# Expert layers of a graph network: first-layer weights split during the attention, new places for the weight tiles, and the best experts found by maximum and first index

## The chip, the cores and the metric

The kernel runs on one core of one Trainium2 chip. The metric is the device time of that core in microseconds. The kernel before takes 1104.51 us (median of three runs, 1102.79 to 1106.34). The core's engines run side by side and meet at semaphores: TensorE (PE in the profile) multiplies matrices, VectorE (DVE), ScalarE (ACT) and GpSimd (POOL) work on vectors, and SyncE (SP) issues transfers. GpSimd also issues the indirect transfers, which gather and scatter rows by an index.

## What is computed

Four blocks act in turn on x, 1024 nodes by 512 features, each on the normalised rows and each added to x. The second and the fourth end in a mixture of eight experts. For these the change alters how the work is ordered; of what is computed only the choice of the experts is written in another way.

```python
x = x + _L0_gnn_ref(_layernorm(x), ...)   # masked attention over 1024 nodes
x = x + _L0_ffn_ref(_layernorm(x), ...)   # experts, the best 2 of 8
x = x + _L1_gnn_ref(_layernorm(x), ...)   # sum over neighbours, two layers
x = x + _L1_ffn_ref(_layernorm(x), ...)   # 8-head attention, then experts, the best 1 of 8

# experts of L0
raw_weights = softmax(flat_x @ gate_w + gate_b)
top_w, top_idx = top_k(raw_weights, 2)
h = gelu(einsum('td,edh->teh', flat_x, w1) + b1)       # w1: 8 x 512 x 256
expert_out = einsum('teh,ehd->ted', h, w2) + b2        # w2: 8 x 256 x 512
combined = einsum('ted,te->td', expert_out, gate_output)
# experts of L1
idx = argmax(t @ Wg + bg)
```

`top_k` and `argmax` take the expert with the lower index where two are equal.

## The kernel before

**Three passes.** A product in full precision is made of three TensorE passes (`three_pass`, L324). Each operand is split into a high part, which is its copy in the rounded type fp32r, and a low part, the operand minus that copy. For the expert weights, `W1R` and `W2R` hold what was loaded (512 KB an expert and layer), `W1H` and `W2H` the high parts, and `W1L` and `W2L` the low parts, written over what was loaded. ScalarE makes the high parts (`w1_hi`, `w2_hi`). VectorE makes the low parts (`weights_lo`, recorded as L971), except the first `POOL_LO` of the first layer's, which GpSimd makes (`expert_lo`, L553): 3 in the first expert layer and 6 in the second. One subtraction of an expert's weights is a 128x1024 instruction.

**An expert layer (`moe`) has a head and a loop.** In the head the normalised rows `XN` are transposed on TensorE (`PS`), copied by ScalarE to `LTH`, and subtracted by VectorE to `LTL`. TensorE multiplies them with the split gate weights `gws`, ScalarE copies the logits to `gatesT`, and TensorE transposes them back (`gt_ps`). VectorE then ranks the eight logits of each row: it compares every expert with every other (`cmp4`, five instructions of 128x512 over 8 tiles x 8 x 8), counts, and writes `picked`. TensorE sums `picked` to ranks and totals. VectorE works out from these which slot each row takes, in blocks of 128 rows for one expert each, and writes `gather_i` and `scatter_i`. Only then can GpSimd gather the first rows (`BX`). The loop follows, 23 blocks in the first layer and 15 in the second: transposed rows, first layer (`hidden`), bias (`hidden_bias`, tile `BH`, L1327), gelu, second layer, scatter. TensorE sets its pace.

**The order is written by hand.** Each engine runs its own list, in order; a wait holds back everything behind it on that engine. VectorE's list in a head is: `LTL` x8, in the first layer the low part of `gws`, then `weights_lo(7)`, the gating, one more subtraction ahead of the slots, and the rest (5 in the first layer, 2 in the second) between the slots and the first rows of the loop.

**What lies ahead of the heads.** The first head follows the masked attention, eight tiles of 128 rows, each with a mask and a minimum on VectorE (`SM`, semaphores `m1` and `m2`), an exponential on ScalarE (`PR`), transposes, `PTH` and `PTL`, the product with V on TensorE, and the addition to x (`residual`, L1169). `W1R` lies where the scores `SR` lay, a slice of 4 KB a partition for each expert as for each tile; its loads wait until all eight tiles are masked. The second head follows the 8-head attention. There, normalisation (`norm_root`, L987 to L996, instructions of 128x8) and `scaled_rows` (L1556, L1560) make `XN`. The tile named WH in ScalarE's rows of L931 is the context's high part, which uses part of the weights' room.

## Time and profile before

| | before |
|---|---|
| median of three runs | 1104.51 us |
| the profiled execution | 1104.55 us, its span 1102.8 us |
| TensorE busy | 884.4 us (80% of the span) |
| VectorE busy | 764.6 us (69%) |
| ScalarE busy | 506.7 us (46%) |
| GpSimd busy | 360.4 us (33%) |
| chain that ended last | PE 57%, DVE 34%, ACT 4% |

By stretches (us from the span's start), with the mean granted clock of TensorE as a share of 2.4 GHz:

| stretch | PE busy | DVE busy | clock |
|---|---|---|---|
| 240 to 310, masked attention | 57.13 | 44.19 | 0.95 |
| 310 to 352, head of the first expert layer | 14.35 | 38.42 | 0.64 |
| 352 to 437, its loop | 82.58 | 35.88 | 0.98 |
| 437 to 655, sums over neighbours | 175.54 | 112.35 | 0.87 |
| 655 to 950, 8-head attention | 264.54 | 222.32 | 0.98 |
| 950 to 1008, norm and head of the second expert layer | 19.04 | 50.89 | 0.64 |
| 1008 to 1066, its loop | 54.23 | 27.36 | 0.97 |

A busy engine is not by that the one that sets the time; what does is read from the chain of waits, which goes back from the last instruction to what released it, step by step. In the timelines, a row is a group of like instructions on one engine. The bracket behind it is the time for which the engine had nothing to do before it, and what ended that wait. Records overlap a little: an instruction's own duration is longer than the distance to the next start.

### The profile page before, as it was taken

The page shows a single profiled execution, that of the slowest core. Times are in us where ns is not written, and L with a number is a line of the kernel's source. Part 1 is how long each engine was busy: PE and PEld are TensorE (multiplying, and loading weights), DVE is VectorE, ACT ScalarE, POOL GpSimd, SP SyncE. Part 2 cuts the span into 40 slices and gives each one's busy share as a digit, 9 for nine tenths or more (in the row PEclk, how much of TensorE's full clock was granted, in tenths as well). Part 3 has the DMA queues.
Part 4 walks back from the last instruction along what each step waited for, and adds up shares of the span by engine and source line. Part 5 has one row for each costly group of instructions (what it writes and reads, how often), then busy time and mean ns, then how long its engine had stood idle before and what let it go on. Part 6 is the DMA issues. An engine that isn't in the chain of part 4 may idle for free.

```text
span 1102.8 us, 13781 instructions
## 1 busy us (share of the span) xinstructions
PE 884.4 (80%) x4522; PEld 675.1 (61%) x4522; DVE 764.6 (69%) x1545; ACT 506.7 (46%) x880; POOL 360.4 (33%) x238
## 2 busy tenths in 40 slices
PE   2999998878953999298898789999999888445990
PEld 2877773337742887077686567777777666334860
DVE  8879599886687443856122767787777776895638
ACT  3467527655362554132302146666665655542530
POOL 1000000000023453007330337786785766602520
PEclk9999999999985999589998999999999998966985
DMA  5010000013371444423110320020010230552442
GB/s 157 29 22 1 1 1 1 1 56 137 113 268 48 135 153 143 163 96 102 52 53 14 105 77 1 20 58 20 1 29 20 72 101 1 168 203 63 151 147 90
DMA packets 55523, 84.74 MB, mean 77 GB/s; under 512 B 8976, under 2 KB 31760, under 8 KB 54944
## 3 DMA queue, kind: packets, MB, share of 16 engines
q1 hardware_dynamic: 49376, 63.94, 18.3%
q0 software_dynamic: 6080, 19.93, 5.5%
q8 instruction: 39, 0.64, 0.2%
q14 instruction: 28, 0.23, 0.1%
HBM read 57.11 MB, written 22.54 MB: 72 GB/s over the span
## 4 chain that ended last, share of the span: by engine, by line
PE 57%; DVE 34%; ACT 4%; issue 3%; POOL 1%; DMA 1%; DVEq 0%; ACTq 0%; POOLq 0%
PE PS L324 37%; DVE late_columns L1133 4%; PE PS L1915 3%; PE PS L1930 3%; DVE neg_max L1488 3%; PE PS L1904 3%; DVE APL L971 2%; PE PS L1929 2%; DVE count_rows L1113 2%; PE PS L1823 2%; PE PS L1604 2%; PE PS L1766 2%; DVE early_columns L1133 1%; DVE XN L1004 1%; DVE stats L979 1%
## 5 line engine op out<-in xcount | busy, mean ns | idle before, releaser
L611 POOL TENSOR_SCALAR AP__193<-AP__193,rden 128x1024 f32<-128x1024 f32 x64 | 181.9, 2847 | 86.4 <-DVE rden L1493 85.7
L553 POOL TENSOR_TENSOR W1L<-W1R,W1H 128x1024 fp32r<-128x1024 f32 x9 | 21.0, 2362 | 307.3 <-ACT W1H L643 307.3
L643 ACT ACTIVATE APH<-PS 128x512 fp32r<-128x512 f32 x128 | 71.7, 597 | 70.1 <-PE PS L1915 45.7
L1488 DVE TENSOR_REDUCE neg_max<-PS 128x1 f32<-128x1024 f32 x64 | 78.2, 1222 | 36.9 <-PE PS L1904 36.0
L971 DVE TENSOR_TENSOR APL<-PS,APH 128x512 fp32r<-128x512 f32 x128 | 82.9, 679 | 23.8 <-ACT APH L643 23.5
L324 PE MATMUL PS<-XTH,WH 128*128 128x512 f32 x224 | 81.5, 411 | 4.5 <-DVE XTL L971 4.5
L1915 PE MATMUL PS<-ident,AP__193 128*128 128x128 f32 x512 | 71.2, 281 | 11.6 <-DVE APL L971 10.8
L324 PE MATMUL PS<-XTL,WH 128*128 128x512 f32 x224 | 78.1, 396 | 0.0
L324 PE MATMUL PS<-XTH,WL 128*128 128x512 f32 x224 | 77.8, 394 | 0.0
L1915 PEld LDWEIGHTS PS<-ident,AP__193 128*128 128x128 f32 x512 | 59.9, 144 | 28.3 <-issue 17.2
L914 ACT ACTIVATE AP__193<-PS,neg_max 128x1024 f32<-128x1024 f32 x64 | 71.5, 1117 | 7.3 <-DVE neg_max L1488 6.6
L544 POOL CAST WH<-RAW 128x512 fp32r<-128x512 f32 x30 | 23.7, 789 | 156.2 <-PE PS L324 91.7
L563 POOL DMA_INDIRECT BX<-normalised,gather_i x38 | 40.2, 1057 | 90.0 <-DVE scatter_i L1311 70.6
L1080 DVE SCALAR_TENSOR_TENSOR edge_lanes<-lanes,edge_lane,edge_vals 128x256 f16<-128x256 f16 x136 | 55.6, 478 | 8.0 <-PE PS L1604 8.0
L1583 PE MATMUL PS<-ident,XN 128*128 128x128 f32 x128 | 28.3, 399 | 40.8 <-DVE XN L1004 16.1
L1930 PE MATMUL PS<-APH,AV 128*128 128x512 f32 x128 | 50.9, 398 | 9.9 <-DVE APL L971 9.7
L576 POOL DMA_INDIRECT expert_rows<-BY,scatter_i x38 | 37.4, 985 | 60.5 <-ACT BY L643 60.5
L676 ACT ACTIVATE edge_steps<-blocks,edge_step 128x145 f16<-128x145 f16 x136 | 45.3, 408 | 20.5 <-PE PS L1604 16.9
L1583 PEld LDWEIGHTS PS<-ident,XN 128*128 128x128 f32 x128 | 23.3, 209 | 45.9 <-DVE XN L1004 17.8
L971 DVE TENSOR_TENSOR BHL<-PS,BHH 128x256 fp32r<-128x256 f32 x38 | 16.1, 424 | 50.4 <-ACT BHH L643 50.4
L1133 DVE TENSOR_SCALAR late_columns<-columns,block_rc 128x512 f16<-128x512 f16 x189 | 50.5, 348 | 0.0
L324 PEld LDWEIGHTS PS<-XTH,WH 128*128 128x128 f32 x224 | 42.1, 193 | 13.3 <-POOL WL L546 3.5
(297 smaller groups left out, 2423.4 us busy)
## 6 DMA issues: line engine op xcount, KB each, us to landing
YT<-expert_rows SPq DMA_DIRECT2D x12, 512.0 KB, 6.8
counts<-CT SPq DMA_DIRECT2D x8, 512.0 KB, 4.9
W1R<-in_L_ffn_w SPq DMA_DIRECT2D x8, 512.0 KB, 8.7
W2R<-in_L_ffn_w SPq DMA_DIRECT2D x8, 512.0 KB, 5.3
normalised<-XN SPq DMA_DIRECT2D x2, 2048.0 KB, 8.0
CG<-counts SPq DMA_DIRECT2D x8, 512.0 KB, 3.3
RAW<-in_L_gnn_W SPq DMA_DIRECT2D x16, 256.0 KB, 2.7
W1R<-in_L_ffn_W SPq DMA_DIRECT2D x8, 512.0 KB, 8.6
```

Of the source, the lines that this page charges most:

```text
L324: got = pe.matmul(o, lhs, r, start=first and j == 0, stop=last and j == 2)
L611: gp.tensor_scalar(AP_[:, i % 4, :], AP_[:, i % 4, :], rden[:, i % 4:i % 4 + 1], None, ALU.mult).then_inc(B["norm"], 1)
L643: act.activation(dst, src, Copy, **kw).then_inc(s, 1)
L676: got = act.activation(edge_steps[:, q % 2, j, 0:STEPS_OF], blocks16[:, :], ACT.Sign, bias=edge_step[:, 4 * q + j:4 * q + j + 1])
L914: act.activation(AP_[:, i % 4, :], banks(2 * (i % 2)), ACT.Exp, bias=neg_max[:, i % 4:i % 4 + 1], accum_out=denom[:, i % 4:i % 4 + 1]).the ...
L971: v.tensor_tensor(dst, src, f(hi), ALU.subtract).then_inc(s, 1)
L1080: got = v.scalar_tensor_tensor(out=edge_lanes[:, q % 2, j, :, :], in0=lanes1[:, :].unsqueeze(1).to_broadcast([P, 2, P]), scalar=edge_lane[ ...
L1133: got = v.tensor_scalar(count_columns(k, j), columns16[:, r * HALF:(r + 1) * HALF], block_rc[:, 1, b:b + 1], None, ALU.is_equal)
L1488: v.tensor_reduce(out=neg_max[:, i % 4:i % 4 + 1], in_=banks(2 * (i % 2)), axis=X_AXIS, op=ALU.max, negate=True).then_inc(B["mx"], 1)
L1583: got = pe.transpose(PS[:, t % 4, k * P:(k + 1) * P], src[:, t, k * P:(k + 1) * P], ident[:, :])
L1915: got = pe.transpose(PS[:, 4 + half, k * P:(k + 1) * P], AP_[:, i % 4, c * P:(c + 1) * P], ident[:, :])
L1930: got = pe.matmul(PS[:, 6, :], AV[:, hp % 2, h, k, :], APH[:, k, :], start=k == 0, stop=k == NT - 1)
```

## The change

- **Gate weights.** Their high part (ScalarE) is made in the attention, and their low part (VectorE) before the last two `residual`.
- **Loads.** `W1R[e]` of the first expert layer is loaded once tile e of the attention is masked, rather than all eight after the last.
- **High parts.** In the first layer ScalarE makes `W1H` 0 to 3 between two exponentials of the attention and 4 to 7 right after it. In the second layer it makes 0 to 3 ahead of the last context copy (L931) and 4 to 7 behind it.
- **Homes.** `W1H` of the first layer lies where the attention's weights lay, and `W2H` where `W1H` was. In the second layer both stay.
- **Low parts.** In the first layer VectorE makes its five `W1L` before the last two `residual` (2 and 3). Behind `LTL` stand 2 subtractions (second layer: 3) instead of 7, then one behind `gates`, one ahead of the slots, 3 (4) behind the slots, and the last 1 (2) behind the loop's first two `BTL`. GpSimd makes 3 and 5 of the first layer's, and waits in the first for the last minimum (`m2`).
- **Best experts.** No comparison of all pairs: the maximum, the experts equal to it, times `rank8` (8 down to 1), the maximum of that, and the expert whose rank it is. For the second best, the first is pushed to minus 3.0e38 and the same is done again. Probabilities get their own tile `prob`.
- **Setup.** `rank8` (an iota of 8 elements) takes the place of `lower` (a memset and an affine_select of 64).

The order of instructions shows the moves at three places. First, VectorE at the end of the masked attention (PTL is the low part of the transposed probabilities, X the `residual`, stats and mv its statistics, eps a constant of the next block). Before:

```order
L971 TENSOR_TENSOR PTL<-PS,PTH 128x1024
L1169 SCALAR_TENSOR_TENSOR X<-PS,rden,X 128x512
L979 BN_STATS stats<-X 128x6
L981 BN_AGGR mv<-stats 128x2
L1169 SCALAR_TENSOR_TENSOR X<-PS,rden,X 128x512
L979 BN_STATS stats<-X 128x6
L981 BN_AGGR mv<-stats 128x2
L1400 TENSOR_SCALAR eps_70<-eps_70 128x1
```

And now:

```order
L976 TENSOR_TENSOR PTL<-PS,PTH 128x1024
L976 TENSOR_TENSOR gws<-gw,gws 128x8x8
L976 TENSOR_TENSOR W1L<-W1R,W1H_156 128x1024 x2
L1174 SCALAR_TENSOR_TENSOR X<-PS,rden,X 128x512
L984 BN_STATS stats<-X 128x6
L986 BN_AGGR mv<-stats 128x2
L976 TENSOR_TENSOR W1L<-W1R,W1H_156 128x1024 x3
L1174 SCALAR_TENSOR_TENSOR X<-PS,rden,X 128x512
L984 BN_STATS stats<-X 128x6
L986 BN_AGGR mv<-stats 128x2
```

The gate weights' low part and five subtractions of W1 now stand between the last `PTL` and the last `X`.

Second, VectorE in the second head, from the last `LTL` to the slots (cmp is `cmp4`, best, top and top_key the new small tiles, over the first tile of the slots). Before:

```order
L971 TENSOR_TENSOR LTL<-PS,LTH 128x4x128 x8
L971 TENSOR_TENSOR W1L<-W1R,W1H 128x1024 x2
L971 TENSOR_TENSOR W2L<-W2R,W2H 128x1024 x5
L1214 TENSOR_TENSOR gtmp<-PS,gbias 128x64
L1217 TENSOR_TENSOR gtmp<-PS,gtmp 128x64
L1237 TENSOR_TENSOR cmp_171<-gtmp 128x512
L1238 TENSOR_TENSOR cmp_171<-gtmp 128x512
L1240 TENSOR_TENSOR cmp_171<-cmp_171,lower 128x512
L1242 TENSOR_TENSOR cmp_171<-cmp_171 128x512
L1244 TENSOR_REDUCE gates<-cmp_171 128x64
L1251 TENSOR_SCALAR picked<-gates 128x64
L1256 TENSOR_SCALAR gates<-gates 128x64
```

And now:

```order
L976 TENSOR_TENSOR LTL<-PS,LTH 128x4x128 x8
L976 TENSOR_TENSOR W1L<-W1R,W1H_157 128x1024 x3
L1218 TENSOR_TENSOR gtmp<-PS,gbias 128x64
L1221 TENSOR_TENSOR gtmp<-PS,gtmp 128x64
L1228 TENSOR_REDUCE best<-gtmp 128x8
L1230 TENSOR_TENSOR top<-gtmp,best 128x64
L1235 TENSOR_TENSOR top_key<-top,rank_76 128x64
L1237 TENSOR_REDUCE best<-top_key 128x8
L1272 TENSOR_TENSOR picked<-rank_76,best 128x64
L1273 TENSOR_TENSOR gates<-rank_76,best 128x64
L976 TENSOR_TENSOR W2L<-W2R,W2H_161 128x1024
L1283 TENSOR_TENSOR over<-PS,edges_97 128x64
```

Four of seven subtractions are gone from between LTL and the gating, the five 128x512 instructions are gone, and one subtraction stands behind `gates`.

Third, ScalarE at the end of the 8-head attention (APH is the high part of the transposed probabilities, WH the context's copy). Before:

```order
L643 ACTIVATE APH<-PS 128x4x128 x6
L931 ACTIVATE WH<-PS,BVA 64x512
L643 ACTIVATE W1H<-W1R 128x1024 x8
L648 ACT_TABLE_LOAD
L648 ACTIVATE rstd<-ve 128x8
L643 ACTIVATE LTH<-PS 128x4x128 x8
```

And now:

```order
L647 ACTIVATE APH<-PS 128x4x128 x6
L647 ACTIVATE W1H_157<-W1R 128x1024 x4
L934 ACTIVATE WH<-PS,BVA 64x512
L647 ACTIVATE W1H_157<-W1R 128x1024 x4
L652 ACT_TABLE_LOAD
L652 ACTIVATE rstd<-ve 128x8
L647 ACTIVATE LTH<-PS 128x4x128 x8
```

Four of the copies to `W1H` have moved ahead of the last context copy.

The diff, cut to its core:

```diff
-    STEPS = (37, 22)
-    POOL_LO = (3, 6)
+    STEPS = (42, 21)
+    POOL_LO = (3, 5)
...
-        def load_w1(w1):
+        def load_w1(which, w1):
             for e in range(NEXP):
+                if which == 0:
+                    wait(A["m1"], e + 1)
                 sp.dma_start(W1R[:, e, :, :], w1[e].rearrange("(k p) h -> p k h", p=P)).then_inc(M["w_in"][e // 4], 16)
...
-        wait(A["m1"], NT)
-        load_w1(a["L0_ffn_w1"])
+        load_w1(0, a["L0_ffn_w1"])
...
 
+        wait(A["m2"], NT)
         expert_lo(0)
         expert_rows(0)
...
+        def w1_hi(which, e):
+            act.wait_ge(M["w_in"][e // 4], which * (160, 96)[e // 4] + 64)
+            copy(W1H[which][:, e, :, :], W1R[:, e, :, :], M["w_hi"])
+
         no_edge(0, 0)
         no_edge(0, 1)
         softmax(0, 0)
@@ -759,39 +767,34 @@
         p_hi(0, 0)
         for i in range(NT // 2 - 1):
             no_edge(i + 1, 0)
+            if i == 1:
+                act.wait_ge(cols_in, 16 * 11)
+                copy(gws[:, :, :, 0:NEXP], gw[:, :, :, :], gw_hi)
+            if i == 2:
+                w1_hi(0, 0)
+                w1_hi(0, 1)
             softmax(i + 1, 0)
             p_hi(i, 1)
...
+            if i == 2:
+                w1_hi(0, 2)
+                w1_hi(0, 3)
...
-
-            if which == 0:
-                act.wait_ge(A["m2"], NT)
-                act.wait_ge(A["stored"], 16 * NT)
-            for e in range(4 if which == 0 else NEXP):
-                w1_hi(e)
+                copy(W2H[which][:, e, :, :], W2R[:, e, :, :], M["w_hi"])
+
+            for e in range(4, NEXP):
+                w1_hi(which, e)
             root((1, 4)[which])
-            if which == 0:
-                w1_hi(4)
-                w1_hi(5)
-                act.wait_ge(A["av_ps"], NT)
-                w1_hi(6)
-                w1_hi(7)
             transposed(turn, LTH)
             if which == 0:
-                act.wait_ge(cols_in, 16 * 11)
...
                         v_hi(hp + 1, m - 10)
+        for e in range(4):
+            w1_hi(1, e)
         context_hi(4 * KT - 1)
...
+        low_tasks = [[(1, e) for e in range(POOL_LO[m], NEXP)] + [(2, e) for e in range(NEXP)] for m in range(2)]
+
+        def weights_lo(which, n):
+            for _ in range(n):
+                layer, e = low_tasks[which].pop(0)
+                v.wait_ge(M["w_hi"], 2 * NEXP * which + NEXP * (layer - 1) + e + 1)
+                wl, wr, wh = ((W1L, W1R, W1H[which]), (W2L, W2R, W2H[which]))[layer - 1]
+                lo(wl[:, e, :, :], wr[:, e, :, :], wh[:, e, :, :], M["w_lo_dve"])
+
...
         p_lo(NT // 2 - 1, 1)
+        v.wait_ge(gw_hi, 1)
+        lo(gws[:, :, :, NEXP:2 * NEXP], gw[:, :, :, :], gws[:, :, :, 0:NEXP], gw_ready)
+        weights_lo(0, 2)
         residual(NT // 2 - 1, 0)
+        weights_lo(0, 3)
         residual(NT // 2 - 1, 1)
...
         def moe(turn, which, acc):
             transposed(turn, LTH, LTL)
...
-            weights_lo(7)
+            weights_lo(which, 2 + which)
...
+            order = rank8[:, :].unsqueeze(1).to_broadcast([P, NT, NEXP])
+            own(v.tensor_reduce(out=best[:, 0, :], in_=gtmp[:, :, :], axis=X_AXIS, op=ALU.max))
+            v.wait_ge(M["gate_dve"], steps[0])
+            own(v.tensor_tensor(top[:, :, :], gtmp[:, :, :], wide(best[:, 0, :]), ALU.is_equal))
+            seen = steps[0]
             if which == 0:
-                own(v.tensor_reduce(out=gsum[:, :], in_=gtmp[:, :, :], axis=X_AXIS, op=ALU.max))
+                own(v.tensor_tensor(prob[:, :, :], gtmp[:, :, :], wide(best[:, 0, :]), ALU.subtract))
+            v.wait_ge(M["gate_dve"], seen)
+            own(v.tensor_tensor(top_key[:, :, :], top[:, :, :], order, ALU.mult))
+            v.wait_ge(M["gate_dve"], steps[0])
+            own(v.tensor_reduce(out=best[:, 1, :], in_=top_key[:, :, :], axis=X_AXIS, op=ALU.max))
+            v.wait_ge(M["gate_dve"], steps[0])
+            if which == 0:
+                own(v.tensor_tensor(first[:, :, :], order, wide(best[:, 1, :]), ALU.is_equal))
                 v.wait_ge(M["gate_dve"], steps[0])
-                own(v.tensor_tensor(gtmp[:, :, :], gtmp[:, :, :], wide(gsum[:, :]), ALU.subtract))
+                own(v.scalar_tensor_tensor(out=rest[:, :, :], in0=first[:, :, :], scalar=-3.0e38, in1=gtmp[:, :, :],
+                                           op0=ALU.mult, op1=ALU.add))
+                v.wait_ge(M["gate_dve"], steps[0])
+                own(v.tensor_reduce(out=best[:, 2, :], in_=rest[:, :, :], axis=X_AXIS, op=ALU.max))
+                seen = steps[0]
                 v.wait_ge(M["g_exp"], 1)
-                own(v.tensor_reduce(out=gsum[:, :], in_=gtmp[:, :, :], axis=X_AXIS, op=ALU.add))
+                own(v.tensor_reduce(out=gsum[:, :], in_=prob[:, :, :], axis=X_AXIS, op=ALU.add))
+                v.wait_ge(M["gate_dve"], seen)
+                own(v.tensor_tensor(top[:, :, :], rest[:, :, :], wide(best[:, 2, :]), ALU.is_equal))
+                v.wait_ge(M["gate_dve"], seen + 1)
+                own(v.reciprocal(gsum[:, :], gsum[:, :]))
+                v.wait_ge(M["gate_dve"], seen + 2)
+                own(v.tensor_tensor(top_key[:, :, :], top[:, :, :], order, ALU.mult))
+                v.wait_ge(M["gate_dve"], seen + 3)
+                own(v.tensor_tensor(prob[:, :, :], prob[:, :, :], wide(gsum[:, :]), ALU.mult))
+                v.wait_ge(M["gate_dve"], seen + 4)
+                own(v.tensor_reduce(out=best[:, 3, :], in_=top_key[:, :, :], axis=X_AXIS, op=ALU.max))
                 v.wait_ge(M["gate_dve"], steps[0])
-                own(v.reciprocal(gsum[:, :], gsum[:, :]))
+                own(v.tensor_tensor(second[:, :, :], order, wide(best[:, 3, :]), ALU.is_equal))
                 v.wait_ge(M["gate_dve"], steps[0])
-                own(v.tensor_tensor(gtmp[:, :, :], gtmp[:, :, :], wide(gsum[:, :]), ALU.mult))
-                v.wait_ge(M["gate_dve"], steps[0])
-            shape = [P, NT, NEXP, NEXP]
-            mine = gtmp[:, :, :].unsqueeze(3).to_broadcast(shape)
-            other = gtmp[:, :, :].unsqueeze(2).to_broadcast(shape)
-            own(v.tensor_tensor(cmp4[:, 0], other, mine, ALU.is_gt))
-            own(v.tensor_tensor(cmp4[:, 1], other, mine, ALU.is_equal))
-            v.wait_ge(M["gate_dve"], steps[0])
-            own(v.tensor_tensor(cmp4[:, 1], cmp4[:, 1], lower[:, :, :].unsqueeze(1).to_broadcast(shape), ALU.mult))
-            v.wait_ge(M["gate_dve"], steps[0])
-            own(v.tensor_tensor(cmp4[:, 0], cmp4[:, 0], cmp4[:, 1], ALU.add))
-            v.wait_ge(M["gate_dve"], steps[0])
-            own(v.tensor_reduce(out=gates[:, :, :], in_=cmp4[:, 0], axis=X_AXIS, op=ALU.add))
-            v.wait_ge(M["gate_dve"], steps[0])
-            K_, nb, first = CHOICES[which], BLOCKS[which], which * BLOCKS[0]
+            K_, nb, base = CHOICES[which], BLOCKS[which], which * BLOCKS[0]
             KN = K_ * NT
             mine8 = picked[:, (NT - 1) * NEXP:].rearrange("p (t e) -> p t e", t=NT)
             if which == 0:
                 v.wait_ge(tabled, 4)
-            v.tensor_scalar(mine8, gates[:, :, :], float(K_), None, ALU.is_lt).then_inc(M["routed"], 1)
             if which == 0:
-                v.scalar_tensor_tensor(out=gates[:, :, :], in0=gates[:, :, :], scalar=2.0, in1=gtmp[:, :, :],
-                                       op0=ALU.is_lt, op1=ALU.mult).then_inc(M["gates"], 1)
+                v.tensor_tensor(mine8, first[:, :, :], second[:, :, :], ALU.add).then_inc(M["routed"], 1)
+                v.wait_ge(M["routed"], 1)
+                v.tensor_tensor(gates[:, :, :], prob[:, :, :], mine8, ALU.mult).then_inc(M["gates"], 1)
             else:
...
+                v.tensor_tensor(mine8, order, wide(best[:, 1, :]), ALU.is_equal).then_inc(M["routed"], 1)
+                v.tensor_tensor(gates[:, :, :], order, wide(best[:, 1, :]), ALU.is_equal).then_inc(M["gates"], 1)
+            weights_lo(which, 1)
...
-            weights_lo(len(tasks))
+            weights_lo(which, 3 + which)
...
+            weights_lo(which, len(low_tasks[which]))
```

The other lines follow from these: `f(W1H[which])` and `W2H[which]` for the two homes, `base` for the name `first`, 12 for 13 steps of setup.

## Rows read from the trace of the kernel before

**Rows 1.** Timeline, VectorE, end of the first attention: start us, us, instruction, idle before.

```profile
303.02 0.75 DVE L1169 SCALAR_TENSOR_TENSOR X<-PS,rden,X 128x512 f32<-128x512 f32 x1 [3.04 <-PE PS L324]
...
308.46 0.75 DVE L1169 SCALAR_TENSOR_TENSOR X<-PS,rden,X 128x512 f32<-128x512 f32 x1 [3.74 <-PE PS L324]
```

**Rows 2.** Chain of waits, first expert head: start us, us, what.

```profile
320.91 5.67 DVE W1L L971 x5
```

**Rows 3.** Timeline, VectorE, first head.

```profile
328.78 0.21 DVE L1214 TENSOR_TENSOR gtmp<-PS,gbias 128x64 f32<-128x64 f32 x1
329.03 0.22 DVE L1217 TENSOR_TENSOR gtmp<-PS,gtmp 128x64 f32<-128x64 f32 x1
...
334.33 0.20 DVE L1251 TENSOR_SCALAR picked<-gates 128x64 f16<-128x64 f32 x1
334.44 0.22 DVE L1253 SCALAR_TENSOR_TENSOR gates<-gates,gtmp 128x64 f32<-128x64 f32 x1
335.43 0.23 DVE L1265 TENSOR_TENSOR over<-PS,edges 128x64 f32<-128x64 f32 x1 [0.76 <-PE PS L1744]
...
355.28 0.42 DVE L1327 TENSOR_TENSOR BH<-PS,B 128x256 f32<-128x256 f32 x1 [1.36 <-PE PS L324]
```

**Rows 4.** Timeline, TensorE, first head.

```profile
320.97 0.40 PE L1728 MATMUL PS<-LTH,gws 128*16 128x512 f32 x1 [1.86 <-DVE gws L971]
...
325.52 0.42 PE L1734 MATMUL PS<-ident,gatesT 16*128 16x16 f32 x4 [0.33 <-ACT gatesT L643]
```

**Rows 5.** Timeline, ScalarE, end of the first attention.

```profile
286.32 1.15 ACT L745 ACTIVATE PR<-SM,neg_max 128x1024 f32<-128x1024 f32 x1 [4.28 <-DVE neg_max L1152]
...
296.44 1.02 ACT L643 ACTIVATE PTH<-PS 128x1024 fp32r<-128x1024 f32 x1 [0.50 <-PE PS L1691]
```

**Rows 6.** Timeline, DMA queue of SyncE; DMA issues with median us to landing.

```profile
292.51 8.39 SPq L381 DMA_DIRECT2D W1R<-in_L_ffn_w  x8
...
W1R<-in_L_ffn_w SPq DMA_DIRECT2D x8, 512.0 KB, 8.7
```

**Rows 7.** Timeline, VectorE, second head; line 991 by itself (ns min/median/max).

```profile
959.31 1.21 DVE L987 TENSOR_SCALAR ve<-mv 128x8 f32<-128x8 f32 x1
...
961.04 1.78 DVE L991 SCALAR_TENSOR_TENSOR sq<-inv 128x8 f32<-128x8 f32 x1
962.85 2.26 DVE L994 TENSOR_TENSOR ve<-sq,ve 128x8 f32<-128x8 f32 x1
...
989.65 0.21 DVE L1214 TENSOR_TENSOR gtmp<-PS,gbias 128x64 f32<-128x64 f32 x1
...
993.66 0.20 DVE L1251 TENSOR_SCALAR picked<-gates 128x64 f16<-128x64 f32 x1
...
1000.94 2.35 DVE L971 TENSOR_TENSOR W2L<-W2R,W2H 128x1024 fp32r<-128x1024 f32 x2
...
1011.46 0.42 DVE L1327 TENSOR_TENSOR BH<-PS,B 128x256 f32<-128x256 f32 x1 [2.08 <-PE PS L324]
...
L991 DVE SCALAR_TENSOR_TENSOR sq<-inv x6: 166/167/1780, 15.7 to 1089.0; 128x8 f32<-128x8 f32 x6
```

**Rows 8.** Timeline, GpSimd, second head.

```profile
951.13 13.96 POOL L553 TENSOR_TENSOR W1L<-W1R,W1H 128x1024 fp32r<-128x1024 f32 x6 [8.12 <-ACT W1H L643]
1001.30 1.78 POOL L563 DMA_INDIRECT BX<-normalised,gather_i  x1 [36.21 <-DVE scatter_i L1311]
1003.38 0.95 POOL L563 DMA_INDIRECT BX<-normalised,gather_i  x1 [0.30 <-issue]
```

**Rows 9.** Timeline, ScalarE and TensorE, second head.

```profile
949.28 0.68 ACT L931 ACTIVATE WH<-PS,BVA 64x512 fp32r<-64x512 f32 x1 [4.30 <-PE PS L1930]
949.99 7.69 ACT L643 ACTIVATE W1H<-W1R 128x1024 fp32r<-128x1024 f32 x8
...
984.42 0.89 PE L1734 MATMUL PS<-ident,gatesT 16*128 16x16 f32 x8 [0.30 <-ACT gatesT L643]
```

**Rows 10.** Timeline, VectorE, start of the program.

```profile
4.02 0.30 DVE L1026 TENSOR_SCALAR tile_of<-src_i 128x136 int32<-128x136 int32 x1 [4.02 <-POOL lower L525]
```

More of the change, by code:

```diff
@@ L210, in build @@
     YT = arena("YT", [P, 2, NT, D], F32, 0)
-    cmp4 = arena("cmp4", [P, 2, NT, NEXP, NEXP], F32, 128)
+    top, top_key, first, second, rest, prob = (arena(n, [P, NT, NEXP], F32, 128 + k / 4)
+                                               for k, n in enumerate(("top", "top_key", "first", "second", "rest", "prob")))
+    best = arena("best", [P, 4, NT], F32, 129.5)
     lane_of = arena("lane_of", [P, 2 * NT, P], F16, 132)
```

55 lines of the change are left out of this document (20 added, 35 removed).

## The prediction, made before the changed kernel was run

> **What bounds the kernel now.** I read the stretches first. Both expert heads stand out: TensorE is mostly idle there and VectorE nearly full, while in the loops behind them TensorE is nearly full. So a head costs what VectorE's list costs, and whatever starts the loop earlier moves the end one for one. I then read the chain of waits through the first head. It runs down VectorE's list, the subtractions included: five of W1 stand in it with 5.67 us, 1.13 us each [rows 2]. The timelines of the other engines show what is late once VectorE no longer is [rows 4, 5, 8]. In the second head the first three small instructions of the normalisation stand out, beside GpSimd's six subtractions [rows 7, 8].
>
> **Start of the program.** VectorE's first instruction is released at 4.02 by GpSimd's `lower` [rows 10], which goes. VectorE's small instructions of about that size take 0.2 us [rows 3]; I take -0.2, between 0 and -0.4.
>
> **End of the masked attention.** VectorE is idle 3.04 us before the seventh residual and 3.74 us before the last [rows 1]. The low part of the gate weights and two subtractions (0.2 + 2.27) go into the first gap, three (3.40) into the second. They would be hidden but for two things. GpSimd's three low parts now start at the last tile's minimum, the instruction behind the mask that released the loads at 292.51 [rows 6], so near 294, and last to about 301 at 2.33 us each (13.96 / 6) [rows 8]; VectorE's instructions with two SBUF operands may have to wait for the end of the one under way, until 301. Then VectorE reaches the seventh residual near 303.4 and leaves the third subtraction at 308.5 instead of 308.46. And the last of the eight loads is issued from 292.51 on; ScalarE is free for its last four copies at 297.46 [rows 5, 6]. With the 8.7 us to landing that eight loads in one heap show [rows 6], it would land near 301 and cost about 0.5; alone it should be faster. ScalarE's first four copies (0.96 each, 7.69 / 8) [rows 9] go in pairs into gaps of 4.28 us ahead of an exponential [rows 5]; the copy of the gate weights is smaller. So I take +0.1, between 0 and +0.5. If VectorE had no such gaps, the five would cost 5.67.
>
> **First head, up to the gating.** The last `LTL` ends near 320.8, since seven subtractions of 1.135 (7.95) end at 328.78, where the gating starts [rows 2, 3]. TensorE's logits no longer wait 1.86 us for the gate weights, and the gates were back at 325.94 [rows 4]. The best case is 325.94 - 1.86 = 324.1. The second head has no wait for gate weights: its last `LTL` ends near 989.65 - 7.95 = 981.7 and its gates are back at 985.31, 3.6 behind [rows 7, 9]. I take that distance: 324.4. VectorE has by then done its two subtractions (2.27) and waits 1.3 us. The gating starts 4.4 us earlier; between 2.8 (gates still at 325.94) and 4.7.
>
> **First head, the gating.** From its first instruction to `picked` it took 5.55 us. Now there are 17 instructions before `picked`. Where one needs the one before it, starts are 0.25 apart; where it doesn't, 0.11 [rows 3]. Following the waits in the diff, four of the 17 run beside others, so 13 distances of 0.25 are left, 3.3: -2.25. Were all 17 in a row it would be 4.25, -1.3.
>
> **First head, behind it.** From `picked` to `over` VectorE had 1.10 us, 0.76 of it waiting for TensorE [rows 3]. Now `gates` waits for `picked` and a subtraction follows: 0.25 + 0.12 + 1.13 = 1.5, +0.4. Three subtractions instead of five stand behind the slots, all under the gathers. The first `BH` had 1.36 us of idle time before it, in which the eighth subtraction of W2 (1.13) now goes: 0.
>
> GpSimd's instruction for a gather took 1.78 us while VectorE ran subtractions (1000.94 to 1003.29), and 0.95 right after [rows 7, 8]. The loop needs the second gather, which used to be under subtractions altogether and is now so for its first microsecond. I take -0.3, between 0 and -0.85.
>
> **Second head, normalisation.** GpSimd subtracts from 951.13 to 965.09, in six pieces of 2.33. Three VectorE instructions take 1.21, 1.78 and 2.26 us in that time, where the same kind takes 0.17 elsewhere (line 991, six times), and they end near 960.5, 962.8 and 965.1, where GpSimd's fourth, fifth and sixth pieces end [rows 7, 8]. Now ScalarE starts its copies when its last high part is done, at 949.28 - 4.30 = 944.98; four end near 948.8, before the context copy is due at 949.28 [rows 9]. GpSimd starts at 946 and does five: 946 + 11.65 = 957.6, before 959.31. All three waits go: 1.04 + 1.61 + 2.09 = 4.74. I take -4.7. Were GpSimd late by a piece, two of them would stay (3.7).
>
> **Second head, up to `over`.** Three subtractions (3.4) instead of seven (7.95), and the gates are back 3.6 behind `LTL`, which is now last: 3.6 + 0.05 against 7.95, -4.3. The gating took 4.01 to `picked`; now six distances of 0.26, 1.55: -2.45. `picked` to `over` was about 1.1 here too; with `picked`, `gates` (0.11 each) and a subtraction it is 1.4: +0.3.
>
> **Second head, behind the slots.** Four subtractions instead of two: they last 4.54 us, over the second gather, which was free of them. It takes 1.8 instead of 0.95, so its rows come 0.85 later. Two more stand between the second `BTL` and `BH`. `BTL` ended at 1011.46 - 2.08 = 1009.38 [rows 7]; now 1009.38 + 0.85 + 2.27 = 1012.5 against 1011.46: +1.0. Without the slower gather it is +0.2; with some delay in the transposes besides, +1.5.
>
> Here a rule speaks against the row. The Trainium skill, "SBUF — State Buffer", section "Who interferes with whom", says that a `tensor_tensor` takes only the read side of the port pair shared with GpSimd, and infers that writing descriptors for a GpSimd transfer is not held up by it. By that rule the second gather stays at 0.95: the second head's last term is +0.2, the first head's gather term 0, and the sum comes out 0.5 us lower. The rows show 1.78 beside subtractions and 0.95 without, so I go by the rows.
>
> **The sum.** Start -0.2; attention +0.1; first head -4.4 - 2.25 + 0.4 - 0.3 = -6.55; second head -4.7 - 4.3 - 2.45 + 0.3 + 1.0 = -10.15. Together -16.8. The profiled execution took 1104.55 us (span 1102.8), 0.04 from the median, so 1104.55 - 16.8 = 1087.7. All terms at their good ends give about 1085, all at their bad ends about 1094.
>
> **The rivals.**
> 1. *The wait on GpSimd stays or moves.* If the five subtractions are drawn out by VectorE's work from 946 on, or ScalarE's early copies hold back the context copy, the normalisation still meets GpSimd. For it: the margin is only 1.7 us (957.6 to 959.31). Against it: beside VectorE's additions and statistics after 951, pieces still took 2.33. Price up to 4.7: 1092.4.
> 2. *The attention pays for the five subtractions.* VectorE sets the pace of the masked attention; if they miss the gaps by waiting for GpSimd or for ScalarE, they cost up to 5.67: 1093.4. Against it: the gaps of 3.04 and 3.74.
> 3. *More than worked out.* TensorE's granted clock is 0.64 over both heads, 0.97 over the loops (the table of stretches): between 1.2 and 2.4 GHz, mostly the lower. Shorter pauses may leave less work at it. With the gathers and distances at their good ends (1085) and 1.5 us of that, 1083.5.
> 4. *Slower.* One list, one stall: VectorE's third to fifth W1 subtractions now stand ahead of the last residuals and need ScalarE's copies of experts 4 to 7, which need the last load. If it lands late, residual, normalisation and head all wait, one for one from about 300 on. The kernel is slower than before once that costs over 17 us, a landing more than 24 us behind its issue; at 27 it would be about 1107.5. Against it: 8.7 with eight in a heap [rows 6].
> 5. *The change doesn't do what it says*: `picked` may be no earlier if the gates come back at their old times. Then 4.4 and 4.3 shrink to 2.8 and about 3: 1090.6.
>
> **Chances.** Forecast as worked, 1085.5 to 1090: 0.66. Rivals 1 and 2: 0.10; rival 5: 0.07; rival 3: 0.12; no gain within the noise: 0.02; rival 4: 0.03. The range 1084 to 1092.5 holds the forecast, rival 5, and part of 1 and 3. Anything from 0.3% (3.3 us) can be told from no change: faster 0.95, same 0.02, slower 0.03.
>
> **What would show it.** In the changed profile: both gatings start within 4 us of the last `LTL`, with VectorE idle before the first; 3.3 and 1.6 us from there to `picked`; the normalisation's small instructions at 0.17 with GpSimd finished by 958; residuals of the attention at their old distances; in the second head a second gather near 1.8 us, and `BH` directly behind two subtractions. I am wrong if the residuals come more than 1 us later, if GpSimd is still subtracting when the normalisation begins, or if the heads are shorter and a later stretch gives it back.

## The result, and the profile after

The changed kernel takes 1089.08 us (median of six runs, 1087.22 to 1089.89), beside 1105.42 us for the kernel before in the same comparison: a ratio of 0.984, 95% interval 0.982 to 0.986, or 16.3 us less between the medians. The forecast was 1087.7. Its profiled execution took 1087.22 us (span 1085.4), and that span is 17.4 below the span of before.

**VectorE, end of the first attention and first head of the changed kernel**, from the timeline: start us, us, instruction, idle before. It answers to [rows 1, 3].

```profile
298.43 1.13 DVE L976 TENSOR_TENSOR gws<-gw,gws 128x64 fp32r<-128x64 f32 x1
...
301.76 0.74 DVE L1174 SCALAR_TENSOR_TENSOR X<-PS,rden,X 128x512 f32<-128x512 f32 x1
...
303.36 3.46 DVE L976 TENSOR_TENSOR W1L<-W1R,W1H 128x1024 fp32r<-128x1024 f32 x3
307.00 0.75 DVE L1174 SCALAR_TENSOR_TENSOR X<-PS,rden,X 128x512 f32<-128x512 f32 x1 [0.17 <-PE PS L328]
...
319.09 2.36 DVE L976 TENSOR_TENSOR W2L<-W2R,W2H 128x1024 fp32r<-128x1024 f32 x2 [0.43 <-ACT W2H L647]
322.41 0.23 DVE L1218 TENSOR_TENSOR gtmp<-PS,gbias 128x64 f32<-128x64 f32 x1 [0.96 <-PE PS L1753]
...
325.79 0.22 DVE L1268 TENSOR_TENSOR picked<-first,second 128x64 f16<-128x64 f32 x1
...
327.32 0.22 DVE L1283 TENSOR_TENSOR over<-PS,edges 128x64 f32<-128x64 f32 x1
...
347.16 0.42 DVE L1345 TENSOR_TENSOR BH<-PS,B 128x256 f32<-128x256 f32 x1 [0.28 <-PE PS L328]
```

The three subtractions fill the gap of 3.74 us down to 0.17. The gating has VectorE waiting ahead of it, for TensorE, as in no head of before. The second gather of this head (GpSimd) meets the subtractions, which end at 340.07, for its first 0.97 us only:

```profile
339.10 1.80 POOL L566 DMA_INDIRECT BX<-normalised,gather_i  x1 [0.30 <-issue]
```

The chain of waits of the changed kernel (start us, us, what; the steps of issue are left out) no longer runs down VectorE's subtractions there, as it did in [rows 2]:

```profile
309.55 8.36 DMA W2R<-in_L_ffn_w
317.99 2.96 ACT W2H L647 x3
320.95 0.96 ACT gatesT L647 x2
321.95 0.43 PE PS L1753 x4
```

In this execution it enters by a load of `W2R`, for which ScalarE waited 0.33 us before its copies. In E4 and E12 below ScalarE doesn't wait for that load, and the distance from `XN` to the gating is 12.07 instead of 12.29.

**Second head of the changed kernel**: first GpSimd, then VectorE. It answers to [rows 7, 8].

```profile
939.09 11.76 POOL L556 TENSOR_TENSOR W1L<-W1R,W1H 128x1024 fp32r<-128x1024 f32 x5 [3.79 <-ACT W1H L647]
983.16 1.78 POOL L566 DMA_INDIRECT BX<-normalised,gather_i  x1 [32.31 <-DVE scatter_i L1329]
985.24 1.86 POOL L566 DMA_INDIRECT BX<-normalised,gather_i  x1 [0.30 <-issue]
987.41 0.95 POOL L566 DMA_INDIRECT BX<-normalised,gather_i  x1 [0.30 <-issue]
```

```profile
952.34 0.17 DVE L992 TENSOR_SCALAR ve<-mv 128x8 f32<-128x8 f32 x1 [0.26 <-DMA rows<-in_L_ffn_beta]
...
953.02 0.17 DVE L996 SCALAR_TENSOR_TENSOR sq<-inv 128x8 f32<-128x8 f32 x1
953.22 0.17 DVE L999 TENSOR_TENSOR ve<-sq,ve 128x8 f32<-128x8 f32 x1
...
973.64 0.23 DVE L1218 TENSOR_TENSOR gtmp<-PS,gbias 128x64 f32<-128x64 f32 x1 [0.17 <-PE PS L1753]
...
975.19 0.22 DVE L1272 TENSOR_TENSOR picked<-rank,best 128x64 f16<-128x64 f32 x1
...
976.60 0.22 DVE L1283 TENSOR_TENSOR over<-PS,edges 128x64 f32<-128x64 f32 x1
...
982.79 4.62 DVE L976 TENSOR_TENSOR W2L<-W2R,W2H 128x1024 fp32r<-128x1024 f32 x4
...
991.87 2.35 DVE L976 TENSOR_TENSOR W2L<-W2R,W2H 128x1024 fp32r<-128x1024 f32 x2
994.13 0.42 DVE L1345 TENSOR_TENSOR BH<-PS,B 128x256 f32<-128x256 f32 x1
```

GpSimd ends at 950.85, 1.5 us ahead of the normalisation, whose three small instructions take 0.17 each, not 1.21, 1.78 and 2.26.

The distances between the starts of such instructions, in us. Before was profiled twice and the changed kernel three times in all (E4, E9, E12 below). The last column is what the prediction worked out for the difference:

| from, to (VectorE) | before | changed | worked out |
|---|---|---|---|
| start of the program to its first instruction | 4.02, 4.03 | 3.74, 3.74, 3.93 | -0.2 |
| first masked scores (`SM`) to the last residual | 63.22, 63.21 | 63.22, 64.88, 65.01 | +0.1 |
| last residual to the first `XN` | 3.34, 3.49 | 3.12 in all | - |
| first head: `XN` to the gating | 16.98, 16.96 | 12.29, 12.07, 12.07 | -4.4 |
| gating to `picked` | 5.55, 5.55 | 3.38, 3.37, 3.37 | -2.25 |
| `picked` to `over` | 1.10, 1.09 | 1.53, 1.54, 1.53 | +0.4 |
| `over` to the first `BH` | 19.85, 19.87 | 19.84, 19.90, 19.84 | -0.3 |
| second head: `ve` to `XN` | 6.04, 6.05 | 1.29 in all | -4.7 |
| `XN` to the gating | 24.30, 24.29 | 20.01, 20.67, 20.59 | -4.3 |
| gating to `picked` | 4.01, 4.01 | 1.55, 1.54, 1.55 | -2.45 |
| `picked` to `over` | 1.09, 1.09 | 1.41 in all | +0.3 |
| `over` to the first `BH` | 16.71, 16.78 | 17.53, 17.48, 17.57 | +1.0 |

Most rows repeat within 0.1 us. Five don't. In E12 VectorE's first instruction waited for a load, until 3.93. The 3.34 and 3.49 of before are a wait for GpSimd (see the part on why the prediction was right). The 12.29 is the wait for the load of `W2R` above. The 63.22 is 1.7 to 1.8 longer in two of three profiles, and the 20.01 is 0.6 to 0.7 longer. In these last two, TensorE works at the lower granted clock for part of the stretch: its products for the first tile of the attention start 0.43 us apart for a while in E4 and 0.23 apart in before. From the first residual to the last it is 48.69 to 48.75 us in all 14 profiles of this case, with and without the subtractions among them.

### The profile page after: what moved, and what is told of

Read it like the earlier page. It is cut to its first block, busy times and chain, and to the rows that moved or that the text cites. A ratio compares the mean times of both kernels' runs of the same rounds, so it can differ in the third digit from the quotient of the medians.

```text
span 1085.4 us, 13783 instructions
## 1 busy us (share of the span) xinstructions
PE 881.8 (81%) x4522; PEld 674.3 (62%) x4522; DVE 757.5 (70%) x1550; ACT 507.2 (47%) x880; POOL 357.7 (33%) x236
## 4 chain that ended last, share of the span: by engine, by line
PE 57%; DVE 32%; ACT 4%; issue 3%; DMA 2%; POOL 1%; SPq 0%; DVEq 0%; ACTq 0%; POOLq 0%
PE PS L328 37%; DVE late_columns L1138 4%; DVE neg_max L1507 3%; PE PS L1934 3%; PE PS L1949 3%; DVE APL L976 3%; PE PS L1948 2%; PE PS L1923 2%; DVE count_rows L1118 2%; PE PS L1842 2%; PE PS L1623 2%; PE PS L1785 2%; DVE early_columns L1138 1%; DVE XN L1009 1%; DVE XN L1575 1%
## 5 line engine op out<-in xcount | busy, mean ns | idle before, releaser
L1934 PEld LDWEIGHTS PS<-ident,AP__201 128*128 128x128 f32 x512 | 59.4, 143 | 28.8 <-issue 16.8
L1697 PE MATMUL PS<-late_columns,count_rows 128*128 128x512 f16 x189 | 46.8, 389 | 4.5 <-DVE late_columns L1138 2.5
```

The costliest lines, as they stand in the source:

```text
L1697: got = pe.matmul(PS[:, ds(held[b % 24]), :].rearrange("p a n -> p (a n)"), count_rows[:, b, :], moving, start=False, stop=False, skip_gro ...
L1934: got = pe.transpose(PS[:, 4 + half, k * P:(k + 1) * P], AP_[:, i % 4, c * P:(c + 1) * P], ident[:, :])
```

## The experiments

Medians of one comparison are of one chip. E1 to E4 are one comparison; E9 to E12 are another, on the same chip; E5 to E8 are a third, on a second chip, where the changed kernel itself wasn't run. The kernel before had 1105.86, 1105.59 and 1105.22 us there. Distances in a head are more exact than medians, and most verdicts rest on them.

**E1: the selection alone.** The kernel before with `rank8` and the new gating, all else as it was.

```
-        lower = const("lower", [P, NEXP, NEXP], F32)
+        rank8 = const("rank8", [P, NEXP], F32)
...
+            own(v.tensor_reduce(out=best[:, 0, :], in_=gtmp[:, :, :], axis=X_AXIS, op=ALU.max))
+            own(v.tensor_tensor(top[:, :, :], gtmp[:, :, :], wide(best[:, 0, :]), ALU.is_equal))
...
```

> The kernel before with only the selection by maximum and first index put in; every low part, every weight and context copy stays where it was. If the working of the prediction holds, the stretch from the first gating operation to the picked weights goes from 5.55 to about 3.4 us in the first head and from 4.01 to about 1.6 us in the second, and the start is 0.3 us shorter: about 4.9 us below the kernel before. If the gatings are not what the slots wait for (the rival: the head is paced by its weights), under 1 us goes. In the second head VectorE still meets GpSimd's last piece in the normalisation (1.21, 1.78 and 2.26 us).

1102.77 us, ratio 0.9975 (0.9962 to 0.9988): 2.8 us less by the ratio, 3.1 by the medians, where 4.9 were expected. The heads did what was worked out: 3.36 us to `picked` in the first (-2.19) and 1.54 in the second (-2.47), with the distance ahead of the gating unchanged (16.97 and 24.30), and the start at 3.74. The normalisation still meets GpSimd (VectorE's timeline in E1):

```profile
957.87 1.21 DVE L987 TENSOR_SCALAR ve<-mv 128x8 f32<-128x8 f32 x1
...
959.59 1.78 DVE L991 SCALAR_TENSOR_TENSOR sq<-inv 128x8 f32<-128x8 f32 x1
961.41 2.26 DVE L994 TENSOR_TENSOR ve<-sq,ve 128x8 f32<-128x8 f32 x1
```

So the 4.9 us (the two selections and the start) are gained where they were expected, and about 2 us are given back outside the heads. E9 and E10 look at that.

**E2: five W1 low parts back behind `LTL`.**

```
-        weights_lo(0, 2)
         residual(NT // 2 - 1, 0)
-        weights_lo(0, 3)
         residual(NT // 2 - 1, 1)
...
-            weights_lo(which, 2 + which)
+            weights_lo(which, (7, 3)[which])
```

> The changed kernel with its five W1 low parts of the attention put back behind the transposed layer of the first head (seven subtractions there, none of this layer's ahead of the normalisation). My theory: they cost nothing in the attention, because the last residual's date is set by TensorE (idle 0.17 us before it), and they gate the gatings here: the first gating operation comes about 5 to 6 us after the last transposed copy instead of 3.8, with ScalarE's copies no longer the last to arrive; +3.9 to +4.3 us over the changed kernel. Rival: the gates are paced by ScalarE's copies and TensorE's transposes anyway, so that the subtractions fit beside them: 0 to +0.5 us. Second rival: the attention pays for them, so that putting them back gives time: -2 us.

1094.27 us against 1089.03 in E4: +5.2 us, ratios to before 0.9902 (0.9883 to 0.9922) and 0.9858 (0.9833 to 0.9882). VectorE in E2:

```profile
318.44 5.75 DVE L976 TENSOR_TENSOR W1L<-W1R,W1H 128x1024 fp32r<-128x1024 f32 x5
324.12 2.35 DVE L976 TENSOR_TENSOR W2L<-W2R,W2H 128x1024 fp32r<-128x1024 f32 x2
326.39 0.21 DVE L1216 TENSOR_TENSOR gtmp<-PS,gbias 128x64 f32<-128x64 f32 x1
```

The gating stands directly behind the subtractions, and `XN` to gating is 16.39, 4.1 to 4.3 more than in the changed kernel: the theory. From the first residual to the last it is 48.70, as with the subtractions in the attention: they cost nothing there. Both rivals fall. The median shows some 1 us more than the head.

**E3: ScalarE's first four copies behind the last context copy.**

```
+        context_hi(4 * KT - 1)
         for e in range(4):
             w1_hi(1, e)
-        context_hi(4 * KT - 1)
```

> The changed kernel with ScalarE's first four W1 copies of the second layer put behind its last context copy instead of ahead of it; nothing else. GpSimd, which makes its pieces from those copies, then starts about 4 to 5 us later than at 939.09 and has its last pieces at work when the normalisation of the second head runs. If GpSimd's piece is what holds VectorE's short normalisation operations there, they take 1 to 2.3 us each again instead of 0.17, and the kernel is 3.3 to 4 us slower than the changed one. Rival: what was gained there came from the copies' cost on ScalarE and the context, not from GpSimd's end: 0, or up to 0.5 us faster.

1091.86 us, 2.8 above E4 (ratio 0.987, 0.9851 to 0.989). GpSimd, then VectorE in E3:

```profile
945.20 11.66 POOL L556 TENSOR_TENSOR W1L<-W1R,W1H 128x1024 fp32r<-128x1024 f32 x5 [8.10 <-ACT W1H L647]
```

```profile
953.42 1.17 DVE L992 TENSOR_SCALAR ve<-mv 128x8 f32<-128x8 f32 x1 [0.15 <-DMA rows<-in_L_ffn_beta]
...
955.10 1.78 DVE L996 SCALAR_TENSOR_TENSOR sq<-inv 128x8 f32<-128x8 f32 x1
956.91 0.17 DVE L999 TENSOR_TENSOR ve<-sq,ve 128x8 f32<-128x8 f32 x1
```

The first two small instructions end at 954.59 and 956.88. GpSimd's last two of five pieces, of 2.33 us each (11.66 / 5), end at 954.53 and 956.86. The third instruction, with GpSimd done, takes 0.17. `ve` to `XN` is 3.89 instead of 1.29. So it is GpSimd's piece under way for which VectorE waits, and a GpSimd that ends before the normalisation takes the waits away. The expectation, 3.3 to 4, was at least 0.7 above these 2.6, since two pieces meet the normalisation and not three.

**E4: the changed kernel again.**

> The changed kernel once more, unaltered, as the yardstick for the runs beside it: 1089.1 us within 1 us. It also tells which of the stretches at TensorE's lower granted clock come back at the same place (in the first execution one fell right behind the wait for the second head's slots, some 996 to 999 us). Theory: that one comes back, since it stands behind the same wait; rival: its place is chance, and the steps between slots change by 0.1 us a pass.

1089.03 us, ratio 0.9858 (0.9833 to 0.9882). The first steps from `BH` to `BH` in the second loop, 4.34 and 4.10 us in the first profile, are 3.45 and 3.49 here: the rival, their place is chance. The profiled span is 2.6 us longer all the same (1088.0), 1.7 of it in the first tile of the masked attention.

**E5: six low parts behind the slots, none ahead of `BH`.**

```
-            weights_lo(which, 3 + which)
+            weights_lo(which, (3, 6)[which])
```

> The changed kernel with all six W2 low parts of the second head behind the slots, and none between the transposed batch and the first low part of the slots' layer. Theory: two subtractions stand before that low part (1.23 and 2.35 us with its wait) and hold TensorE; with them in the cover of the gathers it comes about 1 to 2 us earlier, if the gathers are longer than six subtractions: -1 to -2.5 us below the changed kernel, the more if TensorE's lower clock behind the wait goes too. Rival: the batch waits for the last gather, and two subtractions more beside the gathers hold GpSimd's descriptors up by as much as they save: 0 to +1 us.

1086.97 us, ratio 0.984 (0.9816 to 0.9864), which can't be told from the changed kernel's. GpSimd in E5, then VectorE:

```profile
983.92 1.78 POOL L566 DMA_INDIRECT BX<-normalised,gather_i  x1 [32.30 <-DVE scatter_i L1329]
986.01 1.86 POOL L566 DMA_INDIRECT BX<-normalised,gather_i  x1 [0.31 <-issue]
988.17 1.96 POOL L566 DMA_INDIRECT BX<-normalised,gather_i  x1 [0.30 <-issue]
990.44 0.95 POOL L566 DMA_INDIRECT BX<-normalised,gather_i  x1 [0.30 <-issue]
```

```profile
983.56 6.89 DVE L976 TENSOR_TENSOR W2L<-W2R,W2H 128x1024 fp32r<-128x1024 f32 x6
...
994.12 0.42 DVE L1345 TENSOR_TENSOR BH<-PS,B 128x256 f32<-128x256 f32 x1 [1.40 <-PE PS L328]
```

Three gathers are now slow, but the loop's first two slots need only the first two. The fourth, beside the `BTL` subtraction, which has one operand in PSUM, takes 0.95. `scatter_i` to the second `BTL` is 8.55 as in the changed kernel, and `BH` waits for TensorE alone: `over` to `BH` is 16.75 instead of 17.5. The gain is 0.75, short of the 1 to 2.5 expected, whose upper part counted on the clock.

This is within 0.1 of before (16.71 and 16.78), although the second gather is as slow as in the changed kernel. So the slower gather alone costs nearly nothing (E6 and E11, with the same order there, have 16.82 and 17.06); it costs something once two subtractions stand behind the second `BTL`.

**E6: as E5, and two copies of ScalarE ahead of the gates' copy.**

```
-            for e in range(3):
+            for e in range(2 + which):
```

> As the kernel with six low parts behind the slots, and in the first head ScalarE makes only two of its W2 copies ahead of the gates' copy instead of three. In the changed kernel three such copies (0.9 us each) end just as the gates' copy starts, and VectorE's first gating operation waits 0.96 us for TensorE behind it. Theory: the gates come 0.5 to 0.9 us earlier, and the first head is that much shorter: a further -0.5 to -0.9 us. Rival: the third copy is then late for the low part that VectorE makes from it: 0.

1086.98 us, nothing below E5, where 0.5 to 0.9 less was expected. ScalarE in E6:

```profile
318.11 2.01 ACT L647 ACTIVATE W2H<-W2R 128x1024 fp32r<-128x1024 f32 x2
320.00 0.57 ACT L647 ACTIVATE gatesT<-PS 16x512 f32<-16x512 f32 x1
321.26 0.59 ACT L647 ACTIVATE gatesT<-PS 16x512 f32<-16x512 f32 x1 [0.68 <-PE PS L1747]
```

The first half of the gates is copied 0.85 us earlier, but the second half waits for TensorE's products. `XN` to the gating is 12.31, beside 12.07 in E5. ScalarE and TensorE are nearly level there, and shortening one alone gives 0.1 us at most (11.96 in E11 against 12.07 in E12).

**E7: no low part behind the slots.** All six stand between `BTL` and `BH`.

```
-            weights_lo(which, 3 + which)
+            weights_lo(which, (3, 0)[which])
```

> The changed kernel with no W2 low part behind the second head's slots and all six between the transposed batch and the first low part of the slots' layer. This shows the gathers with VectorE idle beside them. Theory (subtractions with two operands in SBUF hold up GpSimd while it writes descriptors): all three gathers take about 0.95 us instead of 1.78, 1.86 and 0.95, so the batch comes about 1.7 us earlier, and the six subtractions (0.6 to 1.2 us each) then stand before the first low part: +2 to +4 us over the changed kernel in all. Rival (they share nothing that the gathers need): gathers 1.78 and 1.86 us as before, and +3.5 to +5.5 us.

1095.13 us, ratio 0.9899 (0.9872 to 0.9926). GpSimd in E7, then VectorE:

```profile
987.32 1.06 POOL L566 DMA_INDIRECT BX<-normalised,gather_i  x1 [32.87 <-DVE scatter_i L1329]
988.68 0.95 POOL L566 DMA_INDIRECT BX<-normalised,gather_i  x1 [0.30 <-issue]
989.94 0.95 POOL L566 DMA_INDIRECT BX<-normalised,gather_i  x1 [0.30 <-issue]
```

```profile
994.54 6.89 DVE L976 TENSOR_TENSOR W2L<-W2R,W2H 128x1024 fp32r<-128x1024 f32 x6
1001.35 0.42 DVE L1345 TENSOR_TENSOR BH<-PS,B 128x256 f32<-128x256 f32 x1
```

With VectorE idle beside them the gathers take 0.95 to 1.06. From `scatter_i` to the second `BTL` it is then 7.07 us. With one gather beside subtractions (before, E1, E9, E10) it is 7.8 to 8.05, and with two (the changed kernel and the others) 8.5 to 8.6: two such gathers together delay the second batch by 1.5 us. The six subtractions then cost what they save and more: `over` to `BH` is 20.58, +3.05. The expectation was +2 to +4 for the whole kernel, and the kernel's ratio is 0.0041 to 0.0059 above those of the changed kernel, 4.5 to 6.5 us: the head alone fits it, the whole time lies above it, near the rival's +3.5 to +5.5. With an interval of 0.0027 to each side the time doesn't decide between the two; the durations of the gathers do, and they are the theory's. Some 1.0 to 1.4 of the excess lie behind that `BH` (89.02 us to VectorE's last instruction against 87.6 to 88.0), where the first steps from `BH` to `BH` are 5.24 and 4.16.

**E8: the gate weights' low part back behind `LTL`.** 

```
-        lo(gws[:, :, :, NEXP:2 * NEXP], gw[:, :, :, :], gws[:, :, :, 0:NEXP], gw_ready)
         weights_lo(0, 2)
...
             transposed(turn, LTH, LTL)
+            if which == 0:
+                v.wait_ge(gw_hi, 1)
+                lo(gws[:, :, :, NEXP:2 * NEXP], gw[:, :, :, :], gws[:, :, :, 0:NEXP], gw_ready)
```

> The changed kernel with the low part of the gate weights put back behind the transposed layer of the first head instead of in the attention. Theory: it stands between the last transposed copy and the gates' matmuls, whose low product needs it, and in the attention it cost nothing: +1.0 to +1.8 us. Rival: the gates' matmuls wait for ScalarE's work anyway: 0 to +0.3 us.

1090.77 us, ratio 0.9889 (0.9854 to 0.9925), too wide to tell. In E8 TensorE waits for it:

```profile
317.34 0.40 PE L1748 MATMUL PS<-LTH,gws 128*16 128x512 f32 x1 [1.80 <-DVE gws L976]
```

`XN` to the gating is 13.72, 1.4 to 1.65 more: the theory. In the attention this instruction takes 1.13 us (298.43, above), and 0.22 here. It ends there at 299.56, with GpSimd's third piece at 299.49, and the last residual is no later.

**E9, E10: before and the selection alone, profiled once more.** The kernels are those of before and of E1.

> The kernel before, profiled once more. The kernel with the selection alone was 2.6 us below the first profile of before where its heads alone are 4.9 us shorter; the rest lies in stretches that the edit does not touch. Theory: such stretches (the first head's slots to the next normalisation, the second head's slots) vary by up to 1.5 us each with the phase of TensorE's granted clock, so that this profile differs from the first by 1 to 3 us in them while both heads keep their lengths within 0.2 us (16.98, 6.65, 19.85 and 30.34, 5.10, 16.71 us). Rival: they repeat within 0.2 us, and the edit itself lengthens them.

> The kernel with the selection alone, profiled once more. Theory of the clock's phase: the 5.25 us between the first two slots of the second head (3.46 in before) is 3.45 to 3.5 us again in this one or moves elsewhere, while the heads stay 2.2 and 2.4 us shorter than before's. Rival: 5.25 us comes back, since the edit causes it.

One execution each: 1108.09 and 1107.01 us (spans 1106.4 and 1105.2). The heads repeat: 5.55 and 4.01 us in E9, 3.37 and 1.53 in E10. The first step from `BH` to `BH` in the second loop is 5.25 us in both, as in E1, and 3.46 in the first profile of before. TensorE's starts there, in E9 and then in the first profile of before:

```profile
1016.20 0.41 PE L324 MATMUL PS<-W1H,BTH 128*128 x1
1016.41 0.41 PE L324 MATMUL PS<-W1L,BTH 128*128 x1
```

```profile
1013.46 0.28 PE L324 MATMUL PS<-W1H,BTH 128*128 x1
1013.58 0.28 PE L324 MATMUL PS<-W1L,BTH 128*128 x1
```

They start 0.21 apart, not 0.12: the lower of the clock's levels for one slot, worth 1.8 us. The theory for E10, that the 5.25 goes or moves, missed; the rival, that the edit causes it, falls too, since before has it in E9. The theory for E9 holds in kind for this step and missed for the other stretch that it named: from the last `BH` of the first loop to the next normalisation it is 34.39 and 34.47 in before, 35.60 and 35.62 in E1 and E10 (granted clock 0.63 against 0.61), and 34.60, 35.28 and 35.25 in the changed kernel. So of the 2 us missing in E1, 1.2 are lost in this stretch. All twelve profiles of other kernels have more there than before's two (34.60 to 35.62); why stays open. The rest is of a size with what two profiles of one kernel differ by: 3.6 us for before, 5.1 for E1.

**E11, E12: the kernel of E6 and the changed kernel on one chip.**

> Six low parts behind the slots and two copies ahead of the gates' copy once more, beside the changed kernel on the same chip. Theory: 0.7 us from the batch that no longer waits (17.5 to 16.8 us) and 0.1 to 0.2 us in the gates: 0.9 us below the changed kernel. Rival: the earlier difference of 2.1 us between medians, on two chips, was real and comes back.

> The changed kernel, as the yardstick on this chip: 1089 us within 1 us. Its second head's slots follow each other at 3.45 us or at 4.1 to 4.4 us, by the clock's phase; the heads keep 4.91 and 2.95 us from first gating operation to the table of blocks.

1087.74 (ratio 0.9851, 0.9828 to 0.9874) and 1088.39 us (0.9851, 0.9831 to 0.987): the same. In the traces `over` to `BH` is 17.06 against 17.57 and `XN` to the gating 11.96 against 12.07. The 2 us between E5 and E4, measured on two chips, didn't come back on one; whether they were the chip or the spread isn't shown. What is left, 0.5 to 0.75 us, the traces show and the times can't confirm. No version that beats the changed kernel by more than that was found.

## Why the prediction was right

The terms add to -16.8. The same distances, first profile against first, add to -17.3: -0.28 at the start, -0.22 before the first `XN`, which I had not foreseen, -6.44 in the first head, -10.36 in the second. E4 and E12 add to -16.9 and -16.7 against that profile of before if the row of the masked attention is left out, and to -15.2 and -14.9 with it, since its first tile ran at the lower clock for a while. So the stages gave what was worked out. The medians of the three comparisons say -16.3, -16.8 and -17.2.

That the first two profiles differ by 17.4, so near the sum, is luck in part: outside these rows they differ by -1.2 us ahead of the masked attention and by +0.7 between the normalisation behind the first loop and that of the second head, and with smaller differences this leaves -0.1 in all. Within the sum two misses of 0.3 cancel, too: the start of the first gating and the gathers.

- **Attention, +0.1: right.** 63.22 on both sides, and E2 shows the five subtractions free there and dear (4.1 to 4.3) in the head. Rival 2 falls. So does rival 4: the last residual waits 0.17 us, for TensorE, and no load.
- **Before the first `XN`, no term: -0.22.** It is the wait for GpSimd once more, which I had read in the second head only. In before, GpSimd's three pieces ran from 303.61 for 7.06 us, to 310.67, and the first small instruction of this normalisation took 0.40 and ended at 310.69 (in the changed kernel 0.17, with GpSimd done at 299.49):

```profile
310.29 0.40 DVE L987 TENSOR_SCALAR ve<-mv 128x8 f32<-128x8 f32 x1
```

- **Start of the gating in the first head, -4.4: right in kind, 0.3 to 0.5 too small.** The gating starts 3.76 us behind the last `LTL` (3.33 and 3.34 in E4 and E12), near the 3.6 taken from the second head. In the first profile the rest is that the last `LTL` ends 0.45 us sooner behind `XN`. ScalarE's list (in before, then in the changed kernel, below) gives a likely cause, which no run tries by itself: its last four copies to `W1H` stood ahead of `LTH` and held it up until 314.63, and they are now made in the attention. Rival 5 falls.

```profile
314.63 2.09 ACT L643 ACTIVATE LTH<-PS 128x512 fp32r<-128x512 f32 x4
```

```profile
311.87 0.60 ACT L647 ACTIVATE LTH<-PS 128x512 fp32r<-128x512 f32 x1 [2.63 <-PE PS L1602]
```

- **The gating, -2.25 and -2.45: right**, -2.17 and -2.46, and E1 gives them alone.
- **Behind the gates, +0.4 and +0.3: right**, +0.43 and +0.32.
- **Gathers of the first head, -0.3: wrong, 0.** The step that failed is "is now so for its first microsecond": I took a gather covered in part to be slowed in part. The second gather took 1.80, as with full cover (1.79 in before). In this case's heads a gather that meets a subtraction in its first microsecond takes 1.78 to 1.96, and the others 0.94 to 1.06. No gather met one in its second half only, so what that would cost isn't shown.
- **Normalisation of the second head, -4.7: right**, -4.75. E3 makes two of the three waits come back with GpSimd's pieces. GpSimd started 13.25 us ahead of the normalisation (939.09 to 952.34), as worked out from before's times (946 to 959.31); the whole kernel is 7 us earlier by then. Rival 1 falls; its margin was 1.5 us, where 1.7 were worked out. That GpSimd has five pieces and not six was not tried by itself.
- **Up to the gating, -4.3: right**, -4.29; 0.6 less where TensorE's first gate products fall at the lower clock (0.43 us apart in place of 0.23). No run puts the four subtractions back here; this term rests on the rows.
- **Behind the slots, +1.0: right in kind**, +0.8. The second `BTL` is 0.7 later (8.55 against 7.84), not 0.85, and the two subtractions stand behind it. It takes both: without the two subtractions the slower gather costs nearly nothing (16.75 in E5), and with them, but `BTL` at its old distance, `BH` would come about 0.1 later than in before (an estimate: 7.84 and the 2.87 from `BTL` to `BH` of the changed kernel, against 7.84 and 2.77).

The Trainium skill's rule against the second gather's delay ("SBUF — State Buffer", "Who interferes with whom") infers that descriptor writing isn't held up by a `tensor_tensor`. E5 and E7 decide against it here: 1.78, 1.86 and 1.96 us beside six subtractions, 1.06, 0.95 and 0.95 with none. Which access of GpSimd is held up, to the descriptors or to the index `gather_i`, isn't shown. The exclusive lock of which this section speaks fits the other waits: E3's small instructions end with GpSimd's pieces within 0.1 us.

Rival 3 named the clock as a gain. No gain shows; the clock is the spread, 1 to 2 us in several places, in either kernel.

## What to carry to other kernels

Where one engine's list sets a stage, work that is ready early belongs into that engine's waits in the stage before; it is free as long as the wait left there stays above zero, and what it saves is bounded by the next engine, which in this head was ScalarE and TensorE at once. Before GpSimd gets a share of VectorE's work, look at what short VectorE instructions come due while it runs: each can cost the rest of GpSimd's piece. Sum such a change stage by stage between fixed instructions; most such distances repeat within 0.1 us where the whole time spreads by 3, and where one doesn't, look at the clock and at the loads in it.
